# A two-layer graph network on one core: edge counts per 16 targets, the visits at the head, VectorE's order around the pair additions, and the update's last layers

## The chip, the core and the metric

The kernel runs on one core of a Trainium2 chip. The time is device microseconds from the first to the last instruction and what lies around it, as the chip reports it for one execution; the lower the better. TensorE is called PE, VectorE DVE, ScalarE ACT, GpSimd POOL and SyncE SP, as in the profile.

## The reference

1024 nodes of 128 values and 32768 edges, sorted by target. The first layer sends a three-layer message along each edge, sums the messages at both ends, and updates the nodes; the second is a graph convolution.

```python
h = jnp.maximum(_layernorm(x, axis=-1), 0.0)
# first layer: node_states = h, edges = edge_attr_64, vertices = (src, dst)
messages = _mlp3(jnp.concatenate([nodes_i, nodes_j, edges], axis=1), mW1, mb1, mW2, mb2, mW3, mb3)
summed = segment_sum(messages, vertices[:, 0], N) + segment_sum(messages, vertices[:, 1], N)
upd_in = jnp.concatenate([node_states, summed, attention], axis=1)
x = x + _mlp3(upd_in, uW1, ub1, uW2, ub2, uW3, ub3)
h = jnp.maximum(_layernorm(x, axis=-1), 0.0)
# second layer, with a loop edge at each node
norm = dinv[row] * dinv[col]                # dinv = rsqrt(number of edges into a node)
out = segment_sum(norm[:, None] * (h @ W)[row], col, N) + b
x = x + gelu(out)
```

## The kernel before

The 256 tiles of 128 edges go through the engines in 64 groups of four tiles. Two tables of node rows, already multiplied by their part of the first weight, are written to memory at the head; POOL then gathers eight blocks of rows a group (four from each table), three groups ahead at most. The order on every engine is written out by hand in its own `group(g, ...)`, and semaphores tie the engines together.

In its turn g, PE runs the second layer of group g, the first layer of group g+1 in two halves (`first_layer`: four products with the edge features, then four transposes that add the gathered rows), a scatter product of group g-1 between them, the messages of group g, and the other three scatters of g-1. The first two transposes wait for DVE's first pair addition, the others for the second (`add_pairs`, line 1080 of the profile). ACT makes the relus, the distances for the incidence matrices (`distance`) and, for each fourth tile, the whole incidence. DVE makes the low halves of split values (`low_first`, `low_messages`, `low_edges`), three incidence comparisons a group (`incidence`, line 1039; tiles 0 and 2 are laid out in rows of 342, tile 1 contiguously), and the one-hots.

The one-hots serve the graph's count matrix for the second layer. A window is 32 targets; its edges lie in at most ten tiles from a first tile that the head works out; for each of these DVE makes one one-hot of the source's low bits (line 1088) and one of target and source block in 258 columns (line 1089), and PE adds their product to a bank (`count_tile`). Five tiles of a window go into each turn, alternating with the transposes. ACT copies the full bank to `ct_sb` (`window_out`), and DVE sums it in two ways (`window_sums`, lines 1108 and 1110) in every second turn. A window with more tiles is visited again by a loop (`more_windows`) behind the last window; the loop runs at least once, and with this graph exactly once.

Behind the loop come the bias of the sums (`add_bias_of_sums`), the update's three layers on PE with DVE and ACT between them, the second normalisation, the neighbour sums (32 products in four runs), the last product, gelu and the stores.

In short DVE's turn g runs so: two pairs of one-hots, comparison of tile 1 of group g-1, both pair additions for g+1, a pair of one-hots, comparison of tile 2, low half of the edge features, first low half of the first layer, a pair of one-hots, second low half, a pair of one-hots, comparison of tile 0 of group g, low messages, and in every second turn the window's sums.

Of the kernel before, what the change touches and what calls it, by code (L numbers as in the profile page):

```python
# [5 lines left out]
P = 128  # L6
# [11 lines left out]
def gnn_preln_kernel(nc, x, src_cols, dst_cols, edge_attr_t, mW1, mb1, mW2, mb2_cols, mW3, mb3,  # L18
# [24 lines left out]
    VT = 10  # L43
    NW = 32
    WD = N // NW
    WK = WD * NC
    KR, KN, KP = 3, 86, 88
# [5 lines left out]
    HOT = 2  # L53
# [9 lines left out]
    with ExitStack() as ctx:  # L63
# [18 lines left out]
        u3_bank = bank[2:4]  # L82
# [77 lines left out]
        oh_key = sb("oh_key", [P, HOT, VT, KR, KP], BF16)  # L160
        ct_sb = sb("ct_sb", [P, NC, N])
        into_part = sb("into_part", [P, N])
        from_part = sb("from_part", [P, NW, NC])
        add_into = sb("add_into", [P, WD])
        add_from = sb("add_from", [P, NC])
        deg_out = sb("deg_out", [P, NC])
        deg_in = sb("deg_in", [P, NC])
# [7 lines left out]
        scale_h = sb("scale_h", [P, NC])  # L175

# [19 lines left out]
        iota_f = ct_sb[:, 0, :]  # L196
# [13 lines left out]
        tail_sb = oh_key[:, :, :, :, :].rearrange("p h t r n -> p (h t r n)").bitcast(F32)  # L210
# [41 lines left out]
        w_out = sem("w_out")  # L252
        w_sums = sem("w_sums")
# [40 lines left out]
        h2n_ready = sem("h2n_ready")  # L294
        passes_ready = sem("passes_ready")
        zero_ready = sem("zero_ready")
        self_added = sem("self_added")
# [23 lines left out]
        LAST_W = 2 * (NW - 1)  # L321

        def made_in(i):

            return 0 <= i and i + 1 < NW

        def summed_in(b, i):

            return b == 0 and 0 <= i < NW
# [76 lines left out]
        def _(pool):  # L406
# [62 lines left out]
            for g in range(1, GROUPS):  # L469
# [4 lines left out]
                for t in range(GT):  # L474
# [3 lines left out]
            pool.wait_ge(ld_w, 16 * 12)  # L478
            nc.gpsimd.tensor_tensor(xb_sb[:, :, :], x_sb[:, :, :],
                                    ub3_all[:, :].unsqueeze(1).broadcast_to([P, NC, D]), ALU.add).then_inc(xb_ready, 1)  # L480

            pool.wait_ge(into_ready, 1)
            diagonal = ct_all[:, 0:(NC - 1) * (N + P)].rearrange("p (s n) -> p s n", n=N + P)[:, :, 0:P]
            nc.gpsimd.tensor_tensor(diagonal, diagonal, ident[:, :].unsqueeze(1).broadcast_to([P, NC - 1, P]), ALU.add)
            diagonal = ct_all[:, (NC - 1) * (N + P):NC * N]
            nc.gpsimd.tensor_tensor(diagonal, diagonal, ident[:, :], ALU.add).then_inc(self_added, 1)


        @block.tensor
        def _(pe):  # L490
# [90 lines left out]
            for k in range(KH * NH):  # L581
                update_of_node(k)

            def first_layer(g, b, n, k, counting):
# [9 lines left out]
                for t in range(GT):  # L594
                    if k == 0 and t % 2 == 0:

                        pe.wait_ge(pair_added, 2 * g + (t // 2 + 1))
                    mm = nc.tensor.matmul(z1t_bank[k][:, t * P:(t + 1) * P], got[:, g % GB, t, 0, part], ident[:, :],  # L598
                                          start=False, stop=True, is_transpose=True, skip_group_check=True)
                    if counting and t in COUNTS_AT[k]:  # L600
                        count_tile(counting[0], counting[1] * (VT // 2) + t - COUNTS_AT[k][0] + k * len(COUNTS_AT[0]))
# [25 lines left out]
            def wait_incidence(g, t):  # L627

                if t < DT:
# [15 lines left out]
            COUNTS_AT = ((0, 1), (0, 1, 2))  # L645

            def counts_of(g):

                w = (g + 1) // 2
                return (w, (g + 1) % 2) if 0 <= w < NW else None  # L650

            def count_tile(w, j):

                if j % (VT // 2) == 0:
                    pe.wait_ge(w_hot, 2 * w + j // (VT // 2) + 1)
                if j == 0:
                    wait(pe, w_out, w)
                mm = nc.tensor.matmul(bank[2][:, 0:KR * KN], oh_low[:, w % HOT, j, :], oh_key[:, w % HOT, j, :, 0:KN],  # L658
                                      start=(j == 0), stop=(j == VT - 1), skip_group_check=True)
                if j == VT - 1:  # L660
                    mm.then_inc(w_psum, 1)

            def more_windows():

                pe.wait_ge(w_out, NW)
                visits = pe.value_load(rows_i[0:1, 2 * NW - 1:2 * NW], min_val=1, max_val=MORE)
                with pe.Fori(0, visits) as v:
                    pe.wait_ge(more_hot, v + 1)
                    nc.tensor.matmul(bank[2][:, 0:KR * KN], oh_low[:, 0, 0, :], oh_key[:, 0, 0, :, 0:KN],
# [10 lines left out]
            def add_bias_of_sums():  # L680

                pe.wait_ge(cb3_ready, 1)
                for c in range(NC):
                    mm = nc.tensor.matmul(acc_bank[c // 4][:, (c % 4) * P:(c % 4 + 1) * P], cb3[:, c, :], ident[:, :],
                                          start=False, stop=(c % 4 == 3), is_transpose=True, skip_group_check=True)
                    if c % 4 == 3:
                        mm.then_inc(sums_ready, 1)

            def group(g, b, i):

                now, nxt, past = exists(g), exists(g + 1), exists(g - 1)
                if now:
                    second_layer(g, b, 0)
                    second_layer(g, b, 1)
                if g == LAST_W + 1:
                    more_windows()
                if nxt:
                    first_layer(g + 1, 1 - b, i + b, 0, counts_of(g))
                if past:
                    scatter(g - 1, 1 - b, 0)  # L700
                if nxt:
                    first_layer(g + 1, 1 - b, i + b, 1, counts_of(g))
                if now:
                    messages(g)
                if g == LAST_W + 1:
                    count_ends()
                if past:
                    scatter(g - 1, 1 - b, 1)
                    scatter(g - 1, 1 - b, 2)
                    scatter(g - 1, 1 - b, 3)  # L710


            turn_starts()
# [3 lines left out]

            pe.wait_ge(rows_ready, 1)
            run_groups(pe, group, FIRST + 1)
            add_bias_of_sums()  # L720
# [15 lines left out]
            def update_third(n):  # L736
                pe.wait_ge(u2_ready, KH * (n + 1))
# [631 lines left out]
```

## Time and profile before

| | us |
|---|---|
| median of three runs | 765.26 (765.11 to 767.28) |
| profiled execution | 768.67 |
| its span, first to last instruction | 766.8 |
| one group of edges in the steady loop | 10.66 |

A row of a timeline shows one instruction or several alike: its start, its duration to the last one's end, engine and line, what it writes and reads, and in brackets how long its engine stood before it and what ended that. Matmuls overlap, so the distance of two starts tells more than a duration. A row without brackets followed its predecessor on its engine at once.

### The profile page before, as it was taken

What the parts mean: (1) busy time and instruction counts of PE and PEld (TensorE: products, weight loads), DVE (VectorE), ACT (ScalarE), POOL (GpSimd) and SP (SyncE); (2) the same over time, 40 slices, a digit from 0 to 9 for tenths busy, and PEclk for the clock granted to TensorE, in tenths of its full rate; (3) what the DMA queues carried; (4) which work ended last, traced back from release to release, by engine and by line L of the source; (5) the groups of instructions that cost most, each with busy time, mean ns of one, the idle gap of its engine ahead of it and who ended that gap; (6) DMA issues with size and microseconds to landing.
All of it is one profiled execution on the core that took longest, in us unless ns stands there. A gap on an engine that the chain in (4) does not pass through costs nothing.

```text
span 766.8 us, 13408 instructions
## 1 busy us (share of the span) xinstructions
PE 741.0 (97%) x4171; PEld 624.5 (81%) x4171; DVE 688.5 (90%) x1444; ACT 650.0 (85%) x839; POOL 540.6 (71%) x533
## 2 busy tenths in 40 slices
PE   7589999999999999999999999999999999999996
PEld 6468888888888888888888888888888888888755
DVE  7869899999999999899998999989999999999765
ACT  3358899999999999999999999999999999998843
POOL 3677777777777777777777777777777777777100
PEclk9789999999999999999999999999999999999999
DMA  8434334444344443344434444344433444442000
GB/s 230 152 115 127 118 112 126 136 125 129 113 124 130 121 133 114 116 134 128 126 109 125 131 131 125 111 123 131 131 122 107 130 135 128 123 118 84 1 0 28
DMA packets 42566, 90.15 MB, mean 118 GB/s; under 512 B 11136, under 2 KB 17920, under 8 KB 42496
## 3 DMA queue, kind: packets, MB, share of 16 engines
q0 software_dynamic: 24576, 67.14, 28.8%
q1 hardware_dynamic: 17920, 22.16, 9.9%
q8 instruction: 33, 0.54, 0.3%
q14 instruction: 37, 0.30, 0.1%
HBM read 86.64 MB, written 2.62 MB: 116 GB/s over the span
## 4 chain that ended last, share of the span: by engine, by line
PE 85%; POOL 7%; issue 2%; DVE 2%; DMA 1%; ACT 1%; DVEq 0%; SPq 0%; POOLq 0%
PE bank L640 29%; PE bank L612 21%; PE bank L622 14%; PE bank L592 7%; PE bank L598 7%; PE bank L658 4%; POOL rows_sb L451 3%; POOL rows_sb L459 3%; PE bank L732 1%; PE bank L777 1%; DMA table_a<-rows_sb 1%; DMA rows_sb<-table_b,ends_i 1%; PE bank L740 1%; PE bank L726 0%; DVE rows_sb L960 0%
## 5 line engine op out<-in xcount | busy, mean ns | idle before, releaser
L459 POOL DMA_INDIRECT rows_sb<-table_b,ends_i x256 | 266.8, 1042 | 78.0 <-issue 78.0
L451 POOL DMA_INDIRECT rows_sb<-table_a,ends_i x256 | 261.4, 1021 | 83.7 <-issue 77.7
L827 ACT ACTIVATE dist<-iota_h,neg_mid 128x1026 f16<-128x1026 f16 (+1 forms) x256 | 294.1, 1150 | 0.0
L1039 DVE TENSOR_SCALAR ring<-dist,half_gap,times 128x1026 fp32r<-128x1026 f16 (+1 forms) x192 | 224.7, 1171 | 0.3 <-ACT dist L827 0.3
L640 PE MATMUL bank<-ring,m_hi 128*128 128x512 f32 x512 | 172.8, 419 | 0.1
L640 PE MATMUL bank<-ring,m_lo 128*128 128x512 f32 x512 | 161.6, 397 | 0.0
L612 PE MATMUL bank<-ring,w_hi 128*128 128x512 f32 x512 | 151.3, 397 | 1.4 <-DVE ring L1019 1.4
L814 ACT ACTIVATE h_sb<-bank,b_sb 128x512 f32<-128x512 f32 x128 | 87.5, 684 | 59.1 <-PE bank L612 59.1
L1089 DVE TENSOR_SCALAR oh_key<-iota_h,key_f,minus_base 128x258 bf16<-128x258 f16 x321 | 128.9, 401 | 0.0
L622 PE MATMUL bank<-w_sb,h_sb 128*128 128x128 f32 x1024 | 125.8, 276 | 0.0
L598 PE MATMUL bank<-ident,rows_sb 128*128 128x128 f32 x512 | 114.3, 277 | 8.0 <-DVE rows_sb L1080 8.0
L622 PEld LDWEIGHTS bank<-w_sb,h_sb 128*128 128x128 f32 x1024 | 120.7, 193 | 0.2
L612 PEld LDWEIGHTS bank<-ring,w_hi 128*128 128x128 f32 x512 | 96.9, 190 | 24.6 <-DVE ring L1019 2.0
L640 PEld LDWEIGHTS bank<-ring,m_lo 128*128 128x128 f32 x512 | 97.5, 190 | 23.3
L1019 DVE SCALAR_TENSOR_TENSOR ring<-bank,ring 128x512 fp32r<-128x512 f32 x128 | 88.3, 690 | 26.6 <-ACT ring L808 25.0
L1080 DVE TENSOR_TENSOR rows_sb<-rows_sb 128x512 f32<-128x512 f32 x128 | 84.2, 685 | 25.0 <-DMA rows_sb<-table_b,ends_i 24.9
L640 PEld LDWEIGHTS bank<-ring,m_hi 128*128 128x128 f32 x512 | 87.7, 191 | 11.7 <-issue 0.2
L1088 DVE TENSOR_SCALAR oh_low<-iota_h,low_f 128x128 bf16<-128x128 f16 x321 | 86.5, 270 | 2.4 <-issue 2.3
L808 ACT ACTIVATE ring<-bank 128x512 fp32r<-128x512 f32 x128 | 76.1, 594 | 14.3 <-PE bank L598 14.3
L598 PEld LDWEIGHTS bank<-ident,rows_sb 128*128 128x128 f32 x512 | 70.6, 143 | 20.2 <-DVE rows_sb L1080 10.2
L612 PE MATMUL bank<-ring,w_lo 128*128 128x512 f32 x256 | 80.8, 397 | 0.0
L842 ACT ACTIVATE ring<-dist,times,neg_times 128x1024 fp32r<-128x1024 f16 x64 | 79.5, 1243 | 0.1
(186 smaller groups left out, 783.6 us busy)
## 6 DMA issues: line engine op xcount, KB each, us to landing
e_raw<-edge_attr_t SPq DMA_DIRECT2D x128, 128.0 KB
rows_sb<-table_a,ends_i POOLq DMA_INDIRECT x256, 2.8
rows_sb<-table_b,ends_i POOLq DMA_INDIRECT x256, 2.9
table_a<-rows_sb SPq DMA_DIRECT2D x4, 256.0 KB, 3.5
table_b<-rows_sb SPq DMA_DIRECT2D x4, 256.0 KB, 3.0
x_sb<-x SPq DMA_DIRECT2D x2, 256.0 KB, 3.3
out<-oh_key SPq DMA_DIRECT2D x4, 128.0 KB, 1.8
u_sb<-uW SPq DMA_DIRECT2D x1, 384.0 KB, 5.0
```

What stands on the lines that cost most here:

```text
L451: nc.gpsimd.indirect_dma_start(got[:, b, t, 0, :], None, table_a, bass.IndirectOffsetOnAxis(ap=ends_i[:, 0, tile:tile + 1], axis=0),).then ...
L459: nc.gpsimd.indirect_dma_start(got[:, b, t, 1, :], None, table_b, bass.IndirectOffsetOnAxis(ap=ends_i[:, 1, tile:tile + 1], axis=0),).then ...
L598: mm = nc.tensor.matmul(z1t_bank[k][:, t * P:(t + 1) * P], got[:, g % GB, t, 0, part], ident[:, :], start=False, stop=True, is_transpose=T ...
L612: mm = nc.tensor.matmul(z2_bank[m][:, :], w[:, k, m * P:(m + 1) * P], a[:, b, k, :], start=(n == 0), stop=(n == len(parts) - 1))
L622: mm = nc.tensor.matmul(msg_bank[:, t * D:(t + 1) * D], h2_sb[:, k, t * P:(t + 1) * P], w3_sb[:, k, :], start=(t == 0 and k == 0), stop=(k ...
L640: mm = nc.tensor.matmul(acc_bank[n][:, :], part[:, b, t, :], inc[:, t, n * HB:(n + 1) * HB], start=(is_first(g) and t == 0 and part is m_h ...
L814: nc.scalar.activation(h2_sb[:, m, :], z2_bank[m][:, :], ACT.Relu, bias=b2_sb[:, m:m + 1]).then_inc(h2_ready, 1)
L827: nc.scalar.activation(to, of, ACT.Abs, bias=neg_mid[:, bass.ds(g * GT + t, 1)]).then_inc(dist_ready, 1)
L1019: nc.vector.scalar_tensor_tensor(h1_lo[:, b, k, :], z1t_bank[k][:, :], 0.0, h1_hi[:, b, k, :].bitcast(F32), ALU.max, ALU.subtract).then_in ...
L1039: nc.vector.tensor_scalar(to, of, half_gap[:, tile], times[:, tile], ALU.is_equal, ALU.mult).then_inc(inc_ready, 1)
L1088: nc.vector.tensor_scalar(oh_low[:, slot, j, :], iota_h[:, 0:P], low_f[:, bass.ds(tile, 1)], None, ALU.is_equal)
L1089: return nc.vector.tensor_scalar(oh_key[:, slot, j, :, 0:KN], iota_h[:, 0:KR * KN].rearrange("p (r n) -> p r n", r=KR), key_f[:, bass.ds(t ...
```

## The change

Windows have 16 targets instead of 32: 64 windows of six tiles instead of 32 of ten, and keys of 128 contiguous columns instead of 258 in three rows. A turn counts one window, three turns (16, 33, 48) count two. PE makes a window's six products in a row, between the first layer's second half and the messages. A pair of windows stands in one half of a bank; DVE adds it to `ct_sb` (`pair_out`) and sums it, in every second turn, and ACT's copy is gone. `ct_sb` is set to zero, with the diagonal, by ACT in the head. The visits run in the head, ahead of the loop.

On DVE the fast comparison (tile 1) goes to the turn's start, ahead of the first two pairs of one-hots; the first pair addition follows, then the comparison in rows (tile 2), then the second addition. For the last two groups DVE makes all four incidences, contiguously. The bias of the sums goes ahead of the last group's scatter, which runs by halves of the nodes. In the update the third layer is split by its inner index and into three parts, ACT makes the high half of the second layer's rows straight from `x1_sb` by chunks, DVE adds `ub3`, and the neighbour sums end by halves, the first copied while the second runs. The pieces of the diff stand in the order of the engines: settings, PE, ACT, DVE.

```diff
-    VT = 10
-    NW = 32
+    VT = 6
+    NW = 64
-    HOT = 2
+    HOT = 4
...
+        TWICE = (16, 33, 48)
+        def counted_in(g):
+            first = g + sum(g > x for x in TWICE)
+            found = (first, first + 1) if g in TWICE else (first,)
+            return [w for w in found if 0 <= w < NW]
+        def summed_in(g):
+            found = [w // 2 for w in counted_in(g) if w % 2]
+            return found[0] if found else None
...
+            def count_window(w):
+                pe.wait_ge(w_hot, w + 1)
+                if w % 2 == 0:
+                    wait(pe, w_out, w // 2)
+                at = (w // 2) % 2 * PK + w % 2 * WK
+                for j in range(VT):
+                    mm = nc.tensor.matmul(bank[2][:, at:at + WK], oh_low[:, w % HOT, j, :], oh_key[:, w % HOT, j, :],
+                                          start=(j == 0), stop=(j == VT - 1), skip_group_check=True)
+                mm.then_inc(w_psum, 1)
...
+                if g == GROUPS:
+                    add_bias_of_sums()
+                    last_scatter(g - 1, 1 - b)
+                    return
...
-                if g == LAST_W + 1:
-                    more_windows()
...
+                for w in counted_in(g):
+                    count_window(w)
                 if now:
                     messages(g)
...
+            pe.wait_ge(rows_ready, 1)
+            more_windows()
...
-                if summed_in(b, i):
-                    window_out(i)
+            for c in range(NC):
+                nc.scalar.activation(ct_sb[:, c, :], iota_h[:, 0:N], ACT.Copy, scale=0.0).then_inc(ct_zero, 1)
...
-                if makes:
-                    tile0 = window_tile(i + 1)
-                    one_hots(i + 1, tile0, b, (0, 1))
                 if past:
                     incidence(g - 1, 1)
+                if makes and exists(g):
+                    w = makes[0]
+                    tile0 = window_tile(w)
+                    one_hots(w, tile0, (0, 1))
                 if nxt:
-                    add_pairs(g + 1)
-                if makes:
-                    one_hots(i + 1, tile0, b, (2,))
+                    add_pair(g + 1, 0)
                 if past:
                     incidence(g - 1, 2)
+                if past and all_on_vector(g - 1):
+                    incidence(g - 1, 3)
+                if nxt:
+                    add_pair(g + 1, 1)
...
                 if now:
                     incidence(g, 0)
                     low_messages(g, b)
-                if summed_in(b, i):
-                    window_sums(i)
+                if summed_in(g) is not None:
+                    pair_out(summed_in(g))
+                for more in makes[1 if exists(g) else 0:]:
+                    one_hots(more, window_tile(more), range(VT))
...
+            def pair_out(p):
+                dve.wait_ge(w_psum, 2 * p + 2)
+                counts = ct_sb[:, :, bass.ds(p * PD, PD)]
+                found = bank[2][:, p % 2 * PK:(p % 2 + 1) * PK].rearrange("p (d a) -> p a d", a=NC)
+                nc.vector.tensor_tensor(counts, counts, found, ALU.add).then_inc(w_out, 1)
+                dve.wait_ge(w_out, p + 1)
+                nc.vector.tensor_reduce(into_part[:, bass.ds(p * PD, PD)], counts.rearrange("p a d -> p d a"),
+                                        AX_X, ALU.add)
...
+            more_windows()
             dve.wait_ge(w1e_hi_ready, 1)
```

DVE from the low messages (`m_lo`) of one turn into the next, in a turn that sums: `into_part` and `from_part` are the sums, `ring<-dist` the incidence comparisons, `rows_sb<-rows_sb` the pair additions. Before:

```order
L1025 TENSOR_TENSOR m_lo<-bank,m_hi 128x512
L1108 TENSOR_REDUCE into_part<-ct_sb 128x32
L1110 TENSOR_REDUCE from_part<-ct_sb 128x8
...
L1088 TENSOR_SCALAR oh_low<-iota_h,low_f 128x128
...
L1089 TENSOR_SCALAR oh_key<-iota_h,key_f,minus_base 128x3x86
...
L1039 TENSOR_SCALAR ring<-dist,half_gap,times 128x1024
L1080 TENSOR_TENSOR rows_sb<-rows_sb 128x2x256 x2
...
L1039 TENSOR_SCALAR ring<-dist,half_gap,times 128x1026
```

Now, with the pair's drain (`ct_sb<-ct_sb,bank`) in the place of ACT's copy:

```order
L1068 TENSOR_TENSOR m_lo<-bank,m_hi 128x512
L1158 TENSOR_TENSOR ct_sb<-ct_sb,bank 128x8x32
L1160 TENSOR_REDUCE into_part<-ct_sb 128x32
L1162 TENSOR_REDUCE from_part<-ct_sb 128x8
L1082 TENSOR_SCALAR ring<-dist,half_gap,times 128x1024
...
L1139 TENSOR_SCALAR oh_low<-iota_h,low_f 128x128
...
L1140 TENSOR_SCALAR oh_key<-iota_h,key_f,minus_base 128x128
...
L1131 TENSOR_TENSOR rows_sb<-rows_sb 128x2x256
L1082 TENSOR_SCALAR ring<-dist,half_gap,times 128x1026
L1131 TENSOR_TENSOR rows_sb<-rows_sb 128x2x256
```

The fast comparison (128x1024) went ahead of the one-hots, and the comparison in rows (128x1026) went between the two additions; a third instruction was added to the two sums.

PE in the middle of a turn: transposes of gathered rows (`ident,rows_sb`), counts (`oh_key,oh_low`), one scatter, and the messages (`w_sb,h_sb`). Before:

```order
L598 MATMUL bank<-ident,rows_sb 128x128
L658 MATMUL bank<-oh_key,oh_low 128x258
L598 MATMUL bank<-ident,rows_sb 128x128
L658 MATMUL bank<-oh_key,oh_low 128x258
L598 MATMUL bank<-ident,rows_sb 128x128 x2
L640 MATMUL bank<-ring,m_hi 128x512 x2
L640 MATMUL bank<-ring,m_lo 128x512 x2
L598 MATMUL bank<-ident,rows_sb 128x128
L658 MATMUL bank<-oh_key,oh_low 128x258
...
L622 MATMUL bank<-w_sb,h_sb 128x128 x8
```

Now:

```order
L609 MATMUL bank<-ident,rows_sb 128x128 x4
L651 MATMUL bank<-ring,m_hi 128x512 x2
L651 MATMUL bank<-ring,m_lo 128x512 x2
L609 MATMUL bank<-ident,rows_sb 128x128 x4
L663 MATMUL bank<-oh_key,oh_low 128x128 x6
L631 MATMUL bank<-w_sb,h_sb 128x128 x8
```

The counts left the places between the transposes and stand in one run of six ahead of the messages.

PE behind the last second layer (`w_hi`): the visit's product, the last scatters and the messages. Before:

```order
L612 MATMUL bank<-ring,w_hi 128x512 x2
L666 TENSOR_LOAD rows_i
...
L669 MATMUL bank<-oh_key,oh_low 128x258
...
L640 MATMUL bank<-ring,m_hi 128x512 x2
L640 MATMUL bank<-ring,m_lo 128x512 x2
L622 MATMUL bank<-w_sb,h_sb 128x128 x8
L676 MATMUL bank<-ones_col,into_part 128x1 x8
```

Now:

```order
L621 MATMUL bank<-ring,w_hi 128x512 x2
L651 MATMUL bank<-ring,m_hi 128x512 x2
L651 MATMUL bank<-ring,m_lo 128x512 x2
L631 MATMUL bank<-w_sb,h_sb 128x128 x8
L651 MATMUL bank<-ring,m_hi 128x512 x2
...
L687 MATMUL bank<-ident,cb 128x128 x8
L698 MATMUL bank<-ring,m_hi 128x512
```

The visit's loop is gone from here, and the products that count the ends (`ones_col,into_part`) stand two turns earlier.

## Rows read from the trace of the kernel before

**Rows 1.** The page: busy us, share, instructions; then shares of the last chain.

```profile
PE 741.0 (97%) x4171; PEld 624.5 (81%) x4171; DVE 688.5 (90%) x1444; ACT 650.0 (85%) x839; POOL 540.6 (71%) x533
...
PE 85%; POOL 7%; issue 2%; DVE 2%; DMA 1%; ACT 1%; DVEq 0%; SPq 0%; POOLq 0%
```

**Rows 2.** Timeline of PE: start us, us, line, out<-in, count, [idle before <-releaser].

```profile
684.24 0.62 PE L612 MATMUL bank<-ring,w_hi 128*128 128x512 f32 x2
...
694.90 0.62 PE L612 MATMUL bank<-ring,w_hi 128*128 128x512 f32 x2
...
698.62 0.27 PE L598 MATMUL bank<-ident,rows_sb 128*128 128x128 f32 x1
...
699.06 0.38 PE L598 MATMUL bank<-ident,rows_sb 128*128 128x128 f32 x2
...
700.99 1.95 PE L622 MATMUL bank<-w_sb,h_sb 128*128 128x128 f32 x16
```

**Rows 3.** Timeline of ACT, same group of edges.

```profile
685.83 0.69 ACT L814 ACTIVATE h_sb<-bank,b_sb 128x512 f32<-128x512 f32 x1 [1.00 <-PE bank L612]
...
691.16 1.16 ACT L827 ACTIVATE dist<-iota_h,neg_mid 128x1026 f16<-128x1026 f16 x1
```

**Rows 4.** Timeline of DVE, same group and the start of the next.

```profile
691.31 0.69 DVE L1019 SCALAR_TENSOR_TENSOR ring<-bank,ring 128x512 fp32r<-128x512 f32 x1 [0.45 <-ACT ring L808]
691.91 0.25 DVE L1088 TENSOR_SCALAR oh_low<-iota_h,low_f 128x128 bf16<-128x128 f16 x1
692.07 0.40 DVE L1089 TENSOR_SCALAR oh_key<-iota_h,key_f,minus_base 128x258 bf16<-128x258 f16 x1
692.39 1.33 DVE L1039 TENSOR_SCALAR ring<-dist,half_gap,times 128x1026 fp32r<-128x1026 f16 x1
693.64 0.68 DVE L1025 TENSOR_TENSOR m_lo<-bank,m_hi 128x512 fp32r<-128x512 f32 x1
694.24 0.62 DVE L1108 TENSOR_REDUCE into_part<-ct_sb 128x32 f32<-128x256 f32 x1
...
695.10 0.25 DVE L1088 TENSOR_SCALAR oh_low<-iota_h,low_f 128x128 bf16<-128x128 f16 x1
...
696.05 0.81 DVE L1039 TENSOR_SCALAR ring<-dist,half_gap,times 128x1024 fp32r<-128x1024 f16 x1
696.77 1.29 DVE L1080 TENSOR_TENSOR rows_sb<-rows_sb 128x512 f32<-128x512 f32 x2
```

**Rows 5.** Timeline of DVE, the second addition of the second group.

```profile
45.06 0.69 DVE L1080 TENSOR_TENSOR rows_sb<-rows_sb 128x512 f32<-128x512 f32 x1 [4.33 <-DMA rows_sb<-table_b,ends_i]
```

**Rows 6.** Timeline of DVE, the visit at the end.

```profile
720.42 0.40 DVE L1089 TENSOR_SCALAR oh_key<-iota_h,key_f,minus_base 128x258 bf16<-128x258 f16 x1
...
721.88 0.41 DVE L1152 TENSOR_TENSOR ct_sb<-ct_sb,bank 128x256 f32 x1
722.41 0.19 DVE L1155 TENSOR_TENSOR into_part<-into_part,add_into 128x32 f32 x1
```

**Rows 7.** Timeline of PE, behind the last second layer.

```profile
720.88 0.28 PE L669 MATMUL bank<-oh_key,oh_low 128*128 128x258 bf16 x1 [1.67 <-DVE oh_key L1089]
...
722.82 2.97 PE L622 MATMUL bank<-w_sb,h_sb 128*128 128x128 f32 x16
```

**Rows 8.** Busy us by stretch; the 1.00 or 0.50 is the granted clock.

```profile
714.00:718.00 4.00, 4.00 (x19) 3.25 (x18) 3.09 (x8) 2.75 (x5) 0.00 (x0) 1.00 0.00 0
721.60:724.90 3.30, 3.30 (x14) 3.01 (x13) 2.96 (x8) 1.90 (x2) 1.27 (x1) 0.50 0.00 0
```

**Rows 9.** Timeline of ACT, the first activation of the node update.

```profile
21.72 0.69 ACT L895 ACTIVATE uh_sb<-bank,ub_sb 128x512 f32<-128x512 f32 x1 [7.06 <-PE bank L576]
```

**Rows 10.** Timeline of PE, the waits in the update and behind it.

```profile
748.32 2.05 PE L740 MATMUL bank<-u_sb,rows_sb 128*128 128x128 f32 x16 [0.78 <-ACT rows_sb L911]
...
760.03 2.05 PE L756 MATMUL bank<-gw_sb,cb 128*128 128x128 f32 x16 [0.68 <-ACT cb L924]
```

**Rows 11.** GpSimd: durations (ns, min/median/max) of one line, then its timeline.

```profile
L451 POOL DMA_INDIRECT rows_sb<-table_a,ends_i x256: 942/946/2417, 21.3 to 702.9; - x128
...
696.47 2.42 POOL L451 DMA_INDIRECT rows_sb<-table_a,ends_i  x1 [0.30 <-issue]
```

More of the change, by code:

```diff
@@ L81, in gnn_preln_kernel @@
         u2_bank = [bank[6:8], bank[0:2]]
-        u3_bank = bank[2:4]
+        u3_bank = [bank[2], bank[3], bank[6]]
+        u3_chunks = [range(0, HC), range(HC, HC + 2), range(HC + 2, NC)]
         agg_bank = bank[4:6]
@@ L747, in _ @@
             update_second(1, 0)
-            update_third(0)
+            pe.wait_ge(u2_ready, KH)
+            update_third(0, 0)
+            update_third(0, 1)
             update_second(1, 1)
-            update_third(1)
+            pe.wait_ge(u1_added, KH * NH)
+            pe.wait_ge(zero_ready, 1)
+            for n in range(NH):
+                mm = nc.tensor.matmul(agg_bank[n][:, :], zero_r[:, :], w2_hi[0:1, :, :].rearrange("p k n -> p (k n)"),
+                                      start=True, stop=False, skip_group_check=True)
+            mm.then_inc(agg_pass, 1)
+            pe.wait_ge(u2_ready, KH + 1)
+            update_third(1, 0)
+            update_third(2, 0)
+            pe.wait_ge(u2_ready, KH * NH)
+            update_third(1, 1)
+            update_third(2, 1)
             def times_w(n):
@@ L759, in times_w, with neighbours @@
                         mm.then_inc(xw_psum, 1)
-            pe.wait_ge(u1_added, KH * NH)
-            pe.wait_ge(zero_ready, 1)
-            for n in range(NH):
-                mm = nc.tensor.matmul(agg_bank[n][:, :], zero_r[:, :], w2_hi[0:1, :, :].rearrange("p k n -> p (k n)"),
-                                      start=True, stop=False, skip_group_check=True)
-            mm.then_inc(agg_pass, 1)
+            def neighbours(part, half, c, n):
+                col = (half * HC + c) * N + n * HB
+                return nc.tensor.matmul(agg_bank[n][:, :], part[:, half, c, :], ct_r[:, col:col + HB],
+                                        start=False, stop=False, skip_group_check=True)
             pe.wait_ge(passes_ready, 1)
@@ L868, in group @@
                     relu_second(g, 1)
-                if past:
+                if past and not all_on_vector(g - 1):
                     last_gap(g - 1)
@@ L872, in group @@
                     relu_first(g + 1, 1 - b, 0)
-                if past:
+                if past and not all_on_vector(g - 1):
                     last_incidence(g - 1)
@@ L1242, in _ @@
             low_edges(0, 0)
-            tile0 = window_tile(0)
-            for half in range(2):
-                one_hots(0, tile0, half, range(VT // 2))
-            run_groups(dve, group, FIRST + 1, {1: count_passes, LAST_W: more_windows, LAST_W + 1: degrees})
+            middles()
+            run_groups(dve, group, FIRST + 1, {1: count_passes, LAST_SUM: sum_counts, LAST_SUM + 1: degrees})
             def round_counts(chunks):
```

296 lines of the change are left out of this document (155 added, 141 removed).

## The prediction

> **What bounds the kernel now.** I read the busy shares and the shares of the last chain first [rows 1]. TensorE (PE) is busy in 97% of the span and the chain runs 85% on it, so inside the loop the sum is first of all one of PE's matmuls. VectorE (DVE) at 90% and ScalarE (ACT) at 85% are close behind: what matters for them is not their sum but whether a result reaches PE in time. So I laid one steady group side by side on three engines, with S = 684.24 for the start of its second layer and times counted from S.
>
> PE [rows 2]: the next group starts at 694.90, so a group is 10.66 us. The transposes of the gathered rows start 3.72 after a group's start (698.62), alternate with the old count matmuls every 0.11, and the third one, the first that needs the second pair addition, starts at 699.06, 4.16 after.
>
> ACT [rows 3]: its first relu waits for PE at 1.59 (the 1.00 idle in the row) and from there it runs without a pause; the distance that the row comparison needs starts at 6.92 and ends at 8.08. DVE [rows 4]: the second low half of the first layer waits for ACT and starts at 7.07. From there DVE runs without a gap: low half 0.60, one pair of one-hots 0.16 + 0.32, comparison in rows 1.25, low messages 0.60, two window sums 0.86, two pairs of one-hots 0.95, fast comparison 0.72, then the two additions (1.29 to the end of the second): 7.07 + 6.75 = 13.82. PE wants the second addition at 10.66 + 4.16 = 14.82. **That is 1.0 us of slack**, the smallest in the loop that I found, and the change works just there.
>
> **The change, part by part.** *Count matmuls.* 320 matmuls of 258 columns at 0.11 go, 35.2 us; 384 of 128 columns come, six in a row. The same kind scaled by its columns gives 0.055, the 128-column f32 matmuls of the messages at most 1.95/16 = 0.12 [rows 2]. I take 0.06, near the first, which has the same type: 23.0 us, so 12.2 less. A group without counts is 10.66 - 5 x 0.11 = 10.11, with a new window 10.47. About 1 us of the gain falls into groups 0 to 4, where DVE still waits for gathers (4.33 in one wait [rows 5]) and it buys nothing: 11 less. The Trainium skill (TensorE: Matmul & The Clock Gate, Back-to-back issue gap) gives some 81 ns for a sustained matmul of 128 columns; no run here shows one yet. As an estimate by that page six are 0.49, and the total forecast below would be some 3.5 us higher.
>
> *DVE's path from the low half to the second addition.* This I work out again in the new order, for a group that ends with a drained pair of windows. A new pair of one-hots is 0.16 plus a key of 128 columns, between 0.16 (the low one-hot, as wide) and 0.32 (the key of 258) [rows 4]; I take 0.18, since width alone would take some 0.13 off the latter, so 0.34 a pair. Draining a pair on DVE is the visit's addition from PSUM with its wait, 722.41 - 721.88 = 0.53 [rows 6], and two sums of the old shapes, 0.86: 1.39. Then: 7.07 + 0.60 + 0.68 (two pairs) = 8.35, not before the distance at 8.08; + 1.25 + 0.60 + 1.39 = 11.59; + 0.72 + 0.68 + 0.60 (the first addition, 1.29 - 0.69) = 13.59; + 1.25, the comparison in rows that now stands between the additions, + 0.69 = 15.53. With 0.06 to PE (as from a key's end at 720.82 to its matmul at 720.88 [rows 6, 7]), 15.59.
>
> PE wants it earlier than before: no count stands between the transposes, 10.47 + 3.72 + 0.22 = 14.41. **So PE stands 1.18 us in each group that follows a drained pair.** A group that drains nothing ends its path 1.39 earlier, at 14.20, and follows a longer group; there PE doesn't wait. Two groups take 10.47 + 11.65 = 22.12 against 21.32. ACT's start at 1.59 hangs on PE's second layer, so the loop of waits closes over two groups and nothing catches up later. The work drops on every engine and the time rises, because a 1.25 us comparison and the drain were moved ahead of an addition that had 1.0 us to spare.
>
> How often: 32 pairs are drained. The first falls in the gather-bound start and the last has no one-hots behind it. After groups 15, 32 and 47 six more pairs of one-hots (2.04) stand at the end, 3.22 each; the long group behind each of these hides the drain that follows at once. 24 x 1.18 + 3 x 3.22 = 38.0 us.
>
> *Visits to the head.* At the end PE stands 1.67 for the visit, and its matmul takes 0.28 [rows 7], 2.0 together; behind it the 16 message matmuls take 2.97 against 1.95 in a steady group [rows 2, 7], 1.0 more, and the four scatters ahead of them some 0.6, because the granted clock is at half there (0.50, that is 1.2 for 2.4 GHz) after that pause [rows 8]. All that goes, 3.6, and 0.4 of the wait for the sums' copy, because the bias now comes ahead of the last scatter: 4.0 less. In the head ACT zeroes the counts: eight passes of some 1.05 and two diagonals, some 10 us, where it is idle for 7.06 [rows 9]. That moves the node half of the update some 3 us back and the visit ends about 30 us in; the first gathers land about 34 and the second group's keep DVE waiting until 45 anyway [rows 5], so I cost it at nothing; without that cover it is 3 us.
>
> *Update.* PE's 0.78 of waiting for the last relu takes the first half of the last layer, and the 0.68 between the neighbour sums and the last product goes because the first half is copied while the second still runs [rows 10]: 1.4 less. The addition of the bias to x, 1.2 us on DVE now, lies in the some 4 us in which DVE waits for the update's third layer. POOL loses two additions that lay beside other work. Moving these instructions shifts no queue of DMAs.
>
> *Sum.* 768.67 (profiled execution, span 766.8) - 11 + 38.0 - 4.0 - 1.4 = 790.3, 21.6 more. The median 765.26 lies 3.4 below the profiled time; on it I predict **787 us**. Bounds of this case: the key one-hot at 0.16 or 0.32 moves the path by -0.08 or +0.56, four pairs of it, so -2 or +15 us over 27 waits; the count at 0.055 or 0.12, -1 or +10; an error of 0.2 in the path, 5. Its own range is 772 to 803.
>
> **Rivals.** *The second addition comes in time* (faster). Its mechanism: ACT or DVE runs some row shorter, so the path ends before 14.41. Then only PE's work counts: 765.26 - 11 - 4.0 - 1.4 = 749. It decides from a path shorter by 1.18; the break-even is a wait of 0.4. Against it: the same sum for the kernel before gives 13.82, and its addition ends in the trace just there (696.77 + 1.29 = 698.06, 13.82 after S). For it: the new key is contiguous and I have no row of that form.
>
> *The gathers are what counts.* Gathers run at 0.946 + 0.30, 10.0 us for eight, and single ones take 2.4 us, such as the one at 696.47 that lies over the two additions at 696.77 and ends when the comparison in rows runs [rows 4, 11]. With the additions apart a gather gets in between. If the gathers bounded the loop, a group could fall to PE's 10.47, the same 749 us. Against it: PE stands nowhere in the steady loop, the gathers have 0.66 a group to lose. The Trainium skill (SBUF — State Buffer, on the shared port pair) has VectorE and GpSimd lock each other out for a whole instruction; the row of 2.42 us agrees, and by the rule alone the change should be faster. I count that within the first rival.
>
> *Gathers get later* (slower still): each addition now can hold a gather of its own. If every group lost the longest delay seen, 2.42 - 0.95 = 1.47, a group were 11.47 instead of 11.06, 25 us more: 812. It decides from 1.06 of delay a group.
>
> *It doesn't drain on time*: PE waits for a bank of counts. The drain is a group ahead of its reuse; I give that nothing.
>
> **How the numbers follow.** Forecast 0.68, 772 to 803. Addition in time 0.20 (745 to 755). A smaller wait of about 0.3 to 0.6 each, 757 to 772, 0.07. Late gathers 0.05. Within 0.3%, about what a measurement of this kernel tells from no change, lies a part of the third and of the first: faster 0.21, same 0.05, slower 0.74. The range 748 to 803 leaves out half of the second case, the last one and a little of the forecast.
>
> **What would show it.** In the profile after: PE idle some 1.2 us before the transposes, released by DVE's pair addition, about 27 times, three of them 3 us; group lengths 10.5 and 11.65 in turn; the count matmuls 0.06 apart; DVE gapless from the second low half to the second addition; no wait of PE before the last scatters; the end some 5.4 us shorter. I am wrong if PE doesn't stand before the transposes, or if what it waits for there is a gather.

## The result and the profile after

| | before | after |
|---|---|---|
| median, us | 765.43 (765.11 to 767.28) | 801.06 (797.96 to 802.27) |
| span of the profiled execution | 766.8 | 800.5 |
| start of the first group of edges | 38.5 | 38.3 |
| from there to the start of the last group's second layer | 677.7 | 718.6 |
| from there to the end | 50.6 | 43.6 |

The changed kernel is slower: the ratio is 1.0446, with a 95% interval of 1.0426 to 1.0466. The prediction was 787, with a range of 748 to 803. The head costs nothing, the end gains 7.0 us, and the loop loses 40.9.

The page of the changed kernel, its busy times and the last chain, answers to [rows 1]:

```profile
PE 741.0 (93%) x4235; PEld 621.8 (78%) x4235; DVE 696.0 (87%) x1605; ACT 647.5 (81%) x819; POOL 536.1 (67%) x530
...
PE 41%; DVE 29%; issue 15%; ACT 11%; DVEq 4%; POOL 0%; POOLq 0%
```

TensorE has fallen from 97% to 93% and from 85% of the chain to 41%. DVE now holds 29% of the chain. Its busy time is 696.0 us, before 688.5. These 7.5 us aren't what sets the end: with both moves and the two windows early, below, DVE is busy for 695.1 us and the kernel takes 752. It is the place of the work in time. Who waits for whom stands in the list of waits (us in total, times, longest):

```profile
PE bank L609 <- DVE rows_sb L1131: 40.8, 34, 1.8
...
POOL rows_sb L470 <- PE bank L609: 31.3, 25, 4.7
```

The first row is PE before its transposes, waiting for a pair addition. The second says that the gathers now wait for PE to give buffers back, so they are not what is late.

In every second turn DVE drains a pair of windows behind its low messages; the group of edges that starts then is called here a group behind a drained pair. A steady one, on PE (start us, us, line, out<-in, count, [idle before <-releaser]). Its second layer starts at 279.00, and it answers to [rows 2]; the group before it started at 268.51:

```profile
268.51 0.62 PE L621 MATMUL bank<-ring,w_hi 128*128 128x512 f32 x2
...
279.00 0.62 PE L621 MATMUL bank<-ring,w_hi 128*128 128x512 f32 x2
...
282.69 0.38 PE L609 MATMUL bank<-ident,rows_sb 128*128 128x128 f32 x2
284.17 0.44 PE L609 MATMUL bank<-ident,rows_sb 128*128 128x128 f32 x2 [1.09 <-DVE rows_sb L1131]
284.36 0.71 PE L651 MATMUL bank<-ring,m_hi 128*128 128x512 f32 x2
...
285.82 0.50 PE L663 MATMUL bank<-oh_key,oh_low 128*128 128x128 bf16 x6
286.15 2.00 PE L631 MATMUL bank<-w_sb,h_sb 128*128 128x128 f32 x16
...
290.81 0.62 PE L621 MATMUL bank<-ring,w_hi 128*128 128x512 f32 x2
```

The first two transposes run at 282.69. Two take 0.19 (284.17 to 284.36), so the third could start at 282.88, 3.88 after the group's start, and it starts at 284.17: 1.29 us late. (The 1.09 in its row is less, since it counts from the end of the second transpose.) The group takes 290.81 - 279.00 = 11.81, the one ahead of it 10.49. DVE on the way there, which answers to [rows 4]:

```profile
275.55 0.69 DVE L1062 SCALAR_TENSOR_TENSOR ring<-bank,ring 128x512 fp32r<-128x512 f32 x1 [0.38 <-ACT ring L846]
...
276.54 0.25 DVE L1139 TENSOR_SCALAR oh_low<-iota_h,low_f 128x128 bf16<-128x128 f16 x1
276.71 0.31 DVE L1140 TENSOR_SCALAR oh_key<-iota_h,key_f,minus_base 128x128 bf16<-128x128 f16 x1
276.93 1.33 DVE L1082 TENSOR_SCALAR ring<-dist,half_gap,times 128x1026 fp32r<-128x1026 f16 x1
278.18 0.68 DVE L1068 TENSOR_TENSOR m_lo<-bank,m_hi 128x512 fp32r<-128x512 f32 x1
278.78 0.41 DVE L1158 TENSOR_TENSOR ct_sb<-ct_sb,bank 128x256 f32<-128x256 f32 x1
...
280.08 0.81 DVE L1082 TENSOR_SCALAR ring<-dist,half_gap,times 128x1024 fp32r<-128x1024 f16 x1
...
281.58 0.68 DVE L1131 TENSOR_TENSOR rows_sb<-rows_sb 128x512 f32<-128x512 f32 x1
282.18 1.33 DVE L1082 TENSOR_SCALAR ring<-dist,half_gap,times 128x1026 fp32r<-128x1026 f16 x1
283.43 0.68 DVE L1131 TENSOR_TENSOR rows_sb<-rows_sb 128x512 f32<-128x512 f32 x1
```

From the second low half (275.55, 7.04 after 268.51) to the end of the second addition (284.11, 15.60) DVE has no gap; the wait that ends there is PE's. The comparison in rows at 282.18 stands where [rows 4] had the second addition.

The first of the three groups whose turn makes six more pairs of one-hots (turn 15, for window 17), the group of turn 16, on PE, and its clock (the 0.84 and 0.50 behind the busy times):

```profile
218.24 0.63 PE L621 MATMUL bank<-ring,w_hi 128*128 128x512 f32 x2
...
223.93 0.44 PE L609 MATMUL bank<-ident,rows_sb 128*128 128x128 f32 x2 [1.84 <-DVE rows_sb L1131]
225.78 0.69 PE L609 MATMUL bank<-ident,rows_sb 128*128 128x128 f32 x2 [1.41 <-DVE rows_sb L1131]
226.12 1.20 PE L651 MATMUL bank<-ring,m_hi 128*128 128x512 f32 x2
...
230.10 2.70 PE L631 MATMUL bank<-w_sb,h_sb 128*128 128x128 f32 x16
...
235.43 0.62 PE L621 MATMUL bank<-ring,w_hi 128*128 128x512 f32 x2
```

```profile
222.00:226.00 4.00, 0.75 (x4) 0.42 (x4) 4.00 (x10) 1.18 (x2) 3.15 (x3) 0.84 0.33 98
226.00:230.00 4.00, 4.00 (x22) 3.44 (x21) 2.18 (x6) 2.65 (x4) 3.15 (x3) 0.50 0.49 153
```

PE stands 1.84 and 1.41, and behind that the granted clock is at half until past 230: two products of the scatter take 1.20 where they took 0.71, sixteen of the messages 2.70 where they took 2.00. The third transpose starts 225.78 - 218.24 = 7.54 after the group's start instead of 3.88, 3.66 late. The group takes 235.43 - 218.24 = 17.19.

Group lengths of all kernels, as differences of the second layers' starts on PE (medians; "behind a drained pair" is every second group; with the drain moved, those behind the turn in which it stands now):

| kernel | behind a drained pair | the others | the three turns with two windows | first to last group |
|---|---|---|---|---|
| before | 10.66 | 10.68 | none | 677.7 |
| after | 11.81 | 10.49 | 17.19, 17.17, 16.07 | 718.6 |
| after, comparison moved | 10.56 | 10.49 | 13.24, 13.32, 13.21 | 675.9 |
| after, drain moved | 10.7 | 10.49 | 14.56, 12.95, 12.81 | 677.7 |
| after, two windows early | 11.81 | 10.47 | 9.79, 18.21, 15.61 | 712.3 |
| before, comparison between | 11.02 | 10.69 | none | 689.0 |
| after, both moved | 10.48 | 10.48 | 11.94, 11.90, 11.96 | 667.3 |
| after, both moved, early | 10.49 | 10.49 | 9.78, 15.94, 11.92 | 668.5 |
| after, waits filled | 11.82 | 10.49 | 14.58, 14.51, 14.52 | 712.1 |

### The profile page after: what moved, and what is told of

It reads as the page before. It is cut to its first block, busy times and chain, and to the rows that moved or that the text cites. A ratio compares the mean times of both kernels' runs of the same rounds, so it can differ in the third digit from the quotient of the medians.

```text
span 800.5 us, 13804 instructions
## 1 busy us (share of the span) xinstructions
PE 741.0 (93%) x4235; PEld 621.8 (78%) x4235; DVE 696.0 (87%) x1605; ACT 647.5 (81%) x819; POOL 536.1 (67%) x530
## 4 chain that ended last, share of the span: by engine, by line
PE 41%; DVE 29%; issue 15%; ACT 11%; DVEq 4%; POOL 0%; POOLq 0%
PE bank L651 16%; DVE ring L1082 10%; PE bank L631 8%; PE bank L621 7%; DVE rows_sb L1131 4%; ACT dist L867 4%; PE bank L609 4%; DVE oh_key L1140 3%; ACT ring L846 3%; DVE oh_low L1139 3%; DVE m_lo L1068 2%; ACT dist L873 2%; PE bank L663 2%; DVEq L1136 2%; ACT ring L882 2%
## 5 line engine op out<-in xcount | busy, mean ns | idle before, releaser
L867 ACT ACTIVATE dist<-iota_h,neg_mid 128x1024 f16<-128x1024 f16 (+1 forms) x256 | 294.8, 1153 | 0.0
L1082 DVE TENSOR_SCALAR ring<-dist,half_gap,times 128x1026 fp32r<-128x1026 f16 (+1 forms) x194 | 222.3, 1146 | 5.2 <-ACT dist L867 5.1
L651 PE MATMUL bank<-ring,m_hi 128*128 128x512 f32 x504 | 170.7, 420 | 0.0
L631 PE MATMUL bank<-w_sb,h_sb 128*128 128x128 f32 x1024 | 129.9, 281 | 0.1
L609 PE MATMUL bank<-ident,rows_sb 128*128 128x128 f32 x512 | 87.5, 285 | 40.8 <-DVE rows_sb L1131 40.8
L1140 DVE TENSOR_SCALAR oh_key<-iota_h,key_f,minus_base 128x128 bf16<-128x128 f16 x385 | 125.1, 327 | 0.0
L609 PEld LDWEIGHTS bank<-ident,rows_sb 128*128 128x128 f32 x512 | 65.0, 145 | 68.2 <-DVE rows_sb L1131 51.0
L846 ACT ACTIVATE ring<-bank 128x512 fp32r<-128x512 f32 x128 | 75.8, 593 | 38.3 <-PE bank L609 38.3
L1139 DVE TENSOR_SCALAR oh_low<-iota_h,low_f 128x128 bf16<-128x128 f16 x385 | 99.5, 260 | 1.3 <-issue 1.2
L1131 DVE TENSOR_TENSOR rows_sb<-rows_sb 128x512 f32<-128x512 f32 x128 | 86.9, 679 | 0.7 <-DMA rows_sb<-table_b,ends_i 0.7
L882 ACT ACTIVATE ring<-dist,times,neg_times 128x1024 fp32r<-128x1024 f16 x62 | 76.7, 1238 | 0.0
```

What stands on the lines that cost most here:

```text
L631: mm = nc.tensor.matmul(msg_bank[:, t * D:(t + 1) * D], h2_sb[:, k, t * P:(t + 1) * P], w3_sb[:, k, :], start=(t == 0 and k == 0), stop=(k ...
L651: mm = nc.tensor.matmul(acc_bank[n][:, :], part[:, b, t, :], inc[:, t, n * HB:(n + 1) * HB], start=(is_first(g) and t == 0 and part is m_h ...
L846: nc.scalar.activation(h1_hi[:, b, k, :], z1t_bank[k][:, :], ACT.Relu).then_inc(h1_hi_ready, 1)
L867: nc.scalar.activation(to, of, ACT.Abs, bias=neg_mid[:, bass.ds(g * GT + t, 1)]).then_inc(dist_ready, 1)
L1082: nc.vector.tensor_scalar(to, of, half_gap[:, tile], times[:, tile], ALU.is_equal, ALU.mult).then_inc(inc_ready, 1)
L1131: nc.vector.tensor_tensor(got[:, b, tiles, 0, :], got[:, b, tiles, 0, :], got[:, b, tiles, 1, :], ALU.add).then_inc(pair_added, 1)
```

## The experiments

**The comparison in rows behind both additions.** My theory is that the second addition is late; the rivals are the gathers, and DVE's sum of work.

```diff
-                if past:
-                    incidence(g - 1, 2)
-                if past and all_on_vector(g - 1):
-                    incidence(g - 1, 3)
                 if nxt:
                     add_pair(g + 1, 1)
+                if past:
+                    incidence(g - 1, 2)
+                if past and all_on_vector(g - 1):
+                    incidence(g - 1, 3)
```

> The changed kernel with one move: VectorE's comparison in rows (tile 2) stands behind both pair additions instead of between them. If the late second addition is what costs, the path from the second low half to that addition falls from the measured 15.58 us behind a drained pair to 15.58 - 1.25 = 14.33, against 14.37 at which TensorE wants it: the steady stall of 1.31 us in 24 groups all but goes (31 us), and in the three turns with a second window the wait of 1.84 + 1.41 us falls to some 2.2, perhaps with the slow clock behind it (3 to 11 us): 759 to 767 us, groups of 10.5 us throughout. If the gathers on GpSimd or VectorE's sum of work bound the loop, the order of two instructions changes nothing: 795 to 802 us. If only the drain's length matters (a pair costs what it adds), also about 800.

Measured: 761.99 us (759.91 to 762.88), ratio to before 0.9952 (0.9932 to 0.9972), as expected. Some 39 us come back by one exchange of two instructions on DVE; no work was taken away. A steady group behind a drained pair, on DVE and PE:

```profile
287.08 0.41 DVE L1158 TENSOR_TENSOR ct_sb<-ct_sb,bank 128x256 f32<-128x256 f32 x1
...
289.89 1.28 DVE L1131 TENSOR_TENSOR rows_sb<-rows_sb 128x512 f32<-128x512 f32 x2
```

```profile
287.31 0.62 PE L621 MATMUL bank<-ring,w_hi 128*128 128x512 f32 x2
...
290.99 0.67 PE L609 MATMUL bank<-ident,rows_sb 128*128 128x128 f32 x4
```

The second addition ends at 291.17, where PE wants it at 287.31 + 3.88 = 291.19: the four transposes run at 290.99, 3.68 after the group's start, and take 0.67 instead of 0.60. The wait has all but gone. In the turns with two windows the row of the first wait is the old one, the second has all but gone, and the clock stays at 1.00:

```profile
216.59 0.44 PE L609 MATMUL bank<-ident,rows_sb 128*128 128x128 f32 x2 [1.82 <-DVE rows_sb L1131]
217.20 0.44 PE L609 MATMUL bank<-ident,rows_sb 128*128 128x128 f32 x2 [0.16 <-DVE rows_sb L1131]
```

**The drain behind the second addition.** If it is the length of the path, another instruction taken out of it must do the same.

```diff
                 if nxt:
                     add_pair(g + 1, 1)
+                if summed_in(g - 1) is not None and summed_in(g - 1) < PAIRS - 1:
+                    pair_out(summed_in(g - 1))
...
-                if summed_in(g) is not None:
+                if summed_in(g) == PAIRS - 1:
                     pair_out(summed_in(g))
```

> The changed kernel with another move: the drained pair of windows (the addition from PSUM and the two sums, 1.30 us) stands directly behind the second pair addition of the next turn instead of at the end of its own; the two additions stay apart. If the path to the second addition is what costs, it falls to 15.58 - 1.30 = 14.28 against 14.37 wanted: the same 759 to 767 us as with the comparison moved, from quite another instruction. The 1.30 us then lie ahead of the first low half, which waited 1.01 us for ScalarE in the groups without a stall, so that no later wait should grow by more than 0.3 us. If it is the comparison between the additions as such (a gather or a port lock that it lets in) that costs, this move brings nothing: 795 to 802 us. If the drain only moves the wait on to the first low half: 780 to 800 us, with TensorE waiting for the low half or the relu instead.

Measured: 764.14 us (761.55 to 765.48), ratio 0.9978 (0.9966 to 0.9991), as expected. The comparison still stands between the additions, and 37 us are back. So in the changed kernel neither the comparison nor the drain is the cause by itself, nor a gather that gets in between the additions: either instruction may stay, not both. Groups of 10.6 to 10.8 among those of 10.49 show that this path still has hardly any slack.

**The turns with two windows at the start.** This tests what these turns cost.

```diff
-        TWICE = (16, 33, 48)
+        TWICE = (0, 1, 2)
```

> The changed kernel with the three turns that count two windows put at groups 0, 1 and 2, where VectorE waits for the first gathers, instead of 16, 33 and 48. The trace has 17.19, 17.17 and 16.07 us for the three groups concerned, of which 3.25 us are TensorE's wait and some 2.5 the matmuls at half clock behind it. If that is right, three groups of 11.15 (the mean of a steady pair) take their place: 3 x 11.15 against 50.43, 17.0 us less, up to 3 lost again at the start: 784 to 787 us, and no stretch at half clock in the middle of the loop. If only the wait goes and the clock falls for another reason, 10 us less: 791. If the six further one-hots cost as much at the start, 801 us.

Measured: 795.79 us (795.35 to 796.36), 5.3 less than the changed kernel, not 14 to 17. In the middle the three groups are as short as all others, but groups 1 and 2 grew by 18.21 - 14.79 + 15.61 - 11.60 = 7.4, and 28 steady groups stand behind a drained pair instead of 24, 1.3 each. I had counted on a cover at the start, DVE's wait for gathers of [rows 5]. On PE in this kernel, and on DVE in the changed kernel:

```profile
56.28 0.69 PE L609 MATMUL bank<-ident,rows_sb 128*128 128x128 f32 x2 [4.13 <-DVE rows_sb L1131]
58.13 0.69 PE L609 MATMUL bank<-ident,rows_sb 128*128 128x128 f32 x2 [1.16 <-DVE rows_sb L1131]
```

```profile
42.62 0.69 DVE L1131 TENSOR_TENSOR rows_sb<-rows_sb 128x512 f32<-128x512 f32 x1 [0.69 <-DMA rows_sb<-table_b,ends_i]
```

The 4.33 us in which DVE waited for a gather are 0.69 now. That cover was gone, and the clock falls to half there as well (0.50 from 55 to 59 us).

**Before, with the comparison between the additions.** The one part alone.

```diff
                 if nxt:
-                    add_pairs(g + 1)
-                if makes:
-                    one_hots(i + 1, tile0, b, (2,))
+                    add_pairs(g + 1, (0,))
                 if past:
                     incidence(g - 1, 2)
+                if nxt:
+                    add_pairs(g + 1, (1,))
+                if makes:
+                    one_hots(i + 1, tile0, b, (2,))
...
```

> The kernel before with one move taken from the change: the comparison in rows stands between the two pair additions. My theory: the path from the second low half to the second addition grows from 13.82 to 15.07 us where a window was summed, against 14.82 wanted, so TensorE stands 0.25 us in every second group and not in the others: about 31 x 0.25 = 8 us, 770 to 776 us. The comparison costs only what exceeds the slack of 1.0 us. If the full 1.25 us counted in each group: 63 x 1.25 = 79, 844 us; in every second group 804. If a gather that gets in between the additions helps, 760 to 765 us.

Measured: 779.60 us (778.80 to 781.99), ratio 1.0187 (1.0159 to 1.0216). Every second group is 11.02 instead of 10.66 and the others stay: an instruction of 1.25 us costs 0.36, what the slack of 1.0 doesn't hold. I expected 0.25 and 770 to 776, and missed. The 0.06 from DVE to PE, which I had in the sum for the changed kernel, was missing in this one; the last 0.05 stay open. The groups 11, 27, 43 and 59 are another 0.25 longer. In each of them DVE stands 0.16 to 0.18 for its own issue ahead of a one-hot. The kernel before has three such rows in its loop too, and its groups there take 10.66 to 10.68 like all others; without slack even that seems to show:

```profile
162.76 0.25 DVE L1090 TENSOR_SCALAR oh_low<-iota_h,low_f 128x128 bf16<-128x128 f16 x1 [0.17 <-issue]
```

**Both moves at once, and with the two windows early.** The drain stands behind the second addition, the comparison behind the drain.

> The changed kernel with both moves at once: the comparison in rows behind both pair additions, and the drained pair behind the second addition of the next turn. The path to the second addition then ends 1.25 + 1.30 us earlier than in the changed kernel, at 13.03 against 14.37 wanted, 1.3 us of slack as the kernel before had 1.0. What is left in the run with the comparison alone moved is some 0.05 a group in 57 groups and 2.4 us of waiting in each of the three turns with a second window; the first should go (2.9 us) and the second shrink by 1.25 each (3.7): from 761.99 to 753 to 757 us, below the kernel before by what the changed counts and the changed end save. If what is left there has another cause than this path, 760 to 763 us. If the drain ahead of the first low half makes that late, above 763.

> The same with the turns of two windows at groups 0, 1 and 2. Moved there in the changed kernel they cost 18.21 - 14.79 + 15.61 - 11.60 = 7.4 us in groups 1 and 2, since VectorE waits there only 0.69 us for gathers now, not the 4.33 of the kernel before. With 1.3 us of slack in the path that should be some 5, against some 4.5 for the three in the middle: within 2 us of the kernel with both moves, 752 to 758 us. If the start still had the cover that the trace of the kernel before shows, 4.5 us less: 749 to 751.

Measured: 754.25 us (751.00 to 755.76), ratio 0.9851 (0.9825 to 0.9877), and 752.18 us (751.09 to 752.77), ratio 0.9817 (0.9794 to 0.9839), both as expected. Both beat the kernel before; the two intervals overlap, so which place of the double turns (those with two windows) is better isn't settled. The loop is PE's own work again at 10.48, and the page of the second one reads like [rows 1]:

```profile
PE 727.1 (97%) x4235; PEld 615.6 (82%) x4235; DVE 695.1 (93%) x1605; ACT 640.9 (85%) x819; POOL 523.8 (70%) x530
...
PE 87%; DVE 7%; issue 2%; POOL 1%; DMA 1%; DVEq 1%; ACT 1%; SPq 0%; POOLq 0%
```

**The waits in the double turns filled.** PE multiplies the identity while it waits there, so that it doesn't stand; its operands and results touch nothing that DVE or ACT use at that time.

```diff
                     if k == 0 and t % 2 == 0:
+                        fill(g - 1, 8 if t == 0 else 6)
                         pe.wait_ge(pair_added, 2 * g + (t // 2 + 1))
...
+            def fill(g, times):
+                if g in TWICE:
+                    p = counted_in(g)[0] // 2
+                    pe.wait_ge(w_out, p)
+                    for _ in range(times):
+                        nc.tensor.matmul(bank[2][:, p % 2 * PK:p % 2 * PK + P], ident[:, :], ident[:, :],
+                                         start=True, stop=True, skip_group_check=True)
```

> The changed kernel with further matmuls of the identity on TensorE in its two waits in each of the turns 16, 33 and 48 (eight of about 0.21 us ahead of the first transpose, six ahead of the third; their result is overwritten by the counts), and nothing else. They fill 1.7 of 1.84 and 1.3 of 1.41 us. If the pause is what takes TensorE's granted clock to half behind it, the clock stays at 1.00, the three groups fall from 17.2, 17.2 and 16.1 to some 14.4, and the kernel from 801 to 793 to 795 us. If the half clock has another cause, or if the matmuls behind the waits are late for VectorE and ScalarE rather than by the clock, the three groups stay above 16 us and the time within 2 us of 801.

Measured: 794.13 us (794.04 to 796.04): 6.9 us less than the changed kernel, by adding work, as expected. The three groups lose 2.61, 2.66 and 1.55 us, and the group behind each grows by some 0.4. PE and its clock in the same place:

```profile
221.78 1.95 PE L619 MATMUL bank<-ident 128*128 128x128 f32 x16
223.85 0.44 PE L609 MATMUL bank<-ident,rows_sb 128*128 128x128 f32 x2
224.12 1.50 PE L619 MATMUL bank<-ident 128*128 128x128 f32 x12
...
225.89 0.72 PE L660 MATMUL bank<-ring,m_hi 128*128 128x512 f32 x2
...
232.67 0.63 PE L630 MATMUL bank<-ring,w_hi 128*128 128x512 f32 x2
```

```profile
226.00:230.00 4.00, 4.00 (x39) 3.75 (x38) 3.38 (x11) 3.25 (x4) 3.08 (x4) 1.00 0.50 151
```

The transposes start as late as without the filling (the first 2.29 after the last edge product, the third 4.14; in the changed kernel 2.23 and 4.08), since DVE is as late. But from the first scatter to the next group PE takes 232.67 - 225.89 = 6.78, where it took 235.43 - 226.12 = 9.31. PE has no idle row in either stretch, so the 2.53 us are its matmuls at half clock. The Trainium skill (TensorE: Matmul & The Clock Gate, HAM oscillation) tells of a loop in which TensorE's waits for transfers bring the clock down in every round. The trace agrees in so far as the clock fell behind two waits, which here are waits for DVE, and stayed at 1.00 where matmuls filled them.

## Why the prediction was right in sign and too small in size

*What bounds.* Right. The path from the second low half to the second addition, on DVE, against PE's wish for it: 15.53 was forecast and 15.60 measured, 14.41 forecast as wanted and 282.88 - 268.51 = 14.37 measured. The wait was 1.29 instead of 1.18. Its parts were off both ways: a pair of one-hots is 0.39 (276.54 to 276.93), not 0.34, since the key takes 0.22 and not 0.18; the drain is 1.30 (278.78 to 280.08), not 1.39.

*How often.* Right: 24 steady groups show it. Of the 32 groups behind a drained pair these leave out the first and the last, the three double turns themselves, and the three behind them, whose drain is hidden, as forecast.

*Counts.* 0.33 for six (285.82 to 286.15), 0.055 apart, so 0.36 forecast was a little high. The groups without a wait took 10.49, forecast 10.47. The Trainium skill (TensorE: Matmul & The Clock Gate, Back-to-back issue gap) has some 81 ns for each; the measurement decides against that here.

*The end.* From the last group's second layer to the update's first product 716.26 to 735.19 became 756.93 to 770.16, 5.7 less; 1.7 of it are the count sums, which moved into group 61 and cost as much there. That leaves 4.0, as forecast. The update and what follows became 1.3 shorter against 1.4 forecast, although a new wait took a part of the gain back. It answers to [rows 10]:

```profile
782.99 2.05 PE L757 MATMUL bank<-u_sb,rows_sb 128*128 128x128 f32 x16
...
787.89 2.11 PE L793 MATMUL bank<-ring,m_lo 128*128 128x512 f32 x8 [0.99 <-DVE m_lo L1351]
...
793.73 2.00 PE L786 MATMUL bank<-gw_sb,cb 128*128 128x128 f32 x16
```

The waits of 0.78 and 0.68 are gone, but the 0.20 before the low half's products has become 0.99.

*The head.* Costed at nothing, and it cost nothing: the first group starts at 38.3 instead of 38.5.

*What failed* is the price of the three double turns. The wait itself was nearly right: 3.22 late was forecast, and 3.66 is measured at the third transpose, since six more pairs of one-hots take 2.32 on DVE and not 2.04. But I priced only the wait. [rows 7] and [rows 8] had shown what stands behind a pause of PE, message matmuls at half clock, and I used that as a gain at the end and not as a cost in the loop. Forecast 10.47 + 0.36 + 3.22 = 14.05 a turn, measured 17.19, 17.17 and 16.07: 8.3 us, of which the filling, which left the waits as they were, took 6.8 away; most of the other 1.5 is the longer wait. The rest is the two-group period, 22.31 instead of 22.12, 24 times: 4.6 us. Together they make 12.9 of the 13.9 by which the loop missed the forecast's 27.0, and 1.7 are the moved count sums; the start gave 0.7 back. Smaller differences of either sign, such as a further wait in group 61, are left out of this sum.

*Where luck helped.* The 801 lies inside the stated range, but not for the range's reason: it reached up to 803 by a dearer key one-hot (0.32) and dearer counts (0.12), and these took 0.22 and 0.055. Nor did the work drop on every engine, as the prediction has it: PE is busy for 741.0 us before and after, and DVE for 7.5 more.

*The rivals.* "The second addition comes in time" was not what happened, yet its price of 749 was tested: with both moves the kernel takes 752 to 754. The gathers had not 0.66 us a group to lose before, as the prediction reads from their commonest length. Their means are 1.02 and 1.04 us, with 0.30 between; they follow one another from 21.3 to 702.9 [rows 11], some 10.7 a group, as long as the group itself, and DVE waits for them 21 times (us in total, times, longest):

```profile
DVE rows_sb L1080 <- DMA rows_sb<-table_b,ends_i: 24.9, 21, 4.3
```

Still they are not what made the changed kernel slow. There DVE waits for one once, 0.69, and they wait for PE; with the comparison moved they keep up with groups of 10.49. Nor did the additions apart make them shorter: their means are 1.03 and 1.04.

## What to carry to other kernels

Before moving an instruction on an engine that is not the bottleneck, find the wait of the bottleneck that ends last, add up the path to it from the last point at which the engine itself waited, and compare with the time at which the bottleneck wants it; what is put into the path costs nothing up to the slack and everything beyond it. Price a long wait of TensorE with what can follow it: its matmuls ran at half clock for a while, which here cost 1.5 to 2.7 us behind some 3.2 of waiting. Take the load of a queue from the mean of its rows, not from the commonest one. A cover that is read from the trace of before holds for the kernel before only.

## What the runs showed of the hardware that I had not expected

Whether the clock falls behind a wait can't be told from the wait's length alone. The wait of 1.1 us in the 24 steady groups left the granted clock at 1.00 each time, and so did 1.82 + 0.16 in the run with the comparison moved. Waits of 1.84 + 1.41 took it to half in all three groups. With the drain moved, two groups have the same waits, 0.26 + 1.41 and 0.29 + 1.41; behind the first the clock fell, behind the second it didn't (PE, then its clock behind the busy times):

```profile
212.68 0.44 PE L609 MATMUL bank<-ident,rows_sb 128*128 128x128 f32 x2 [0.26 <-DVE rows_sb L1133]
214.53 0.44 PE L609 MATMUL bank<-ident,rows_sb 128*128 128x128 f32 x2 [1.41 <-DVE rows_sb L1133]
...
396.42 0.44 PE L609 MATMUL bank<-ident,rows_sb 128*128 128x128 f32 x2 [0.29 <-DVE rows_sb L1133]
398.27 0.44 PE L609 MATMUL bank<-ident,rows_sb 128*128 128x128 f32 x2 [1.41 <-DVE rows_sb L1133]
```

```profile
216.00:220.00 4.00, 4.00 (x31) 3.94 (x30) 3.96 (x11) 2.37 (x3) 3.09 (x4) 0.62 0.62 175
...
397.00:401.00 4.00, 2.73 (x26) 2.51 (x27) 3.92 (x9) 2.45 (x5) 3.08 (x4) 1.00 0.22 71
401.00:405.00 4.00, 4.00 (x27) 3.50 (x26) 4.00 (x11) 3.38 (x5) 3.09 (x4) 1.00 0.61 175
```

That is the difference between 14.56 and 12.95 us for the group. The third such group, with 0.17 + 1.41, kept the clock at 1.00 too. Why it falls in one of them stays open.
